# Twelve-layer decoder on one core: Hadamard layer's input levels as sums, cross attentions and latent layers in another order

## The reference, cut to what matters

```python
def _L0_xattn_ref(q, latent_kv, Wq, Wkv_expand, Wout):      # also layer 3
    qp = q @ Wq.T
    kv = latent_kv @ Wkv_expand.T
    k, v = jnp.split(kv, 2, axis=-1)
    # 16 heads of 32, causal softmax
    ...
    return out @ Wout.T

def _L0_ffn_ref(input, SU_ug, SU_dp, Wscale_ug, Wscale_dp, W_up, W_gate, W_down):
    x = fwht(x * SU_ug) / SCALE                             # Walsh-Hadamard transform over 512
    x_up = x @ W_up.T * (Wscale_ug[:INTER] * SCALE)
    x_gate = x @ W_gate.T * (Wscale_ug[INTER:] * SCALE)
    x = jax.nn.silu(x_gate) * x_up
    x = fwht(x * SU_dp) / SCALE                             # and over 2048
    x = x @ W_down.T * (Wscale_dp * SCALE)

def _L2_xattn_ref(hidden_q, kv_c, Wq, w_kc_q, w_kc_kv, W_qr, W_kr, Wo):   # layer 1 has no rope on q_big
    q_hk = (hidden_q @ Wq.T).reshape(Bv, Sv, H, K)          # 16 heads of 128
    q_big = jnp.einsum('bshk,hkq->bshq', q_hk, w_kc_q)      # 384 wide
    q_big = _apply_rope(q_big, ...)
    q_r = jnp.einsum('bshq,hqr->bhsr', q_big, W_qr)         # 64 wide
    k_r = jnp.einsum('bld,hdr->bhlr', kv_r, W_kr)
    attn = jax.nn.softmax(jnp.einsum('bhsr,bhlr->bhsl', q_r, k_r), axis=-1)
    ctx_c = jnp.einsum('bhsl,bld->bhsd', attn, kv_r)
    ctx_lat = jnp.einsum('bhsd,hkd->bhsk', ctx_c, w_kc_kv)
    return ctx_lat.transpose(0, 2, 1, 3).reshape(Bv, Sv, H * K) @ Wo.T
```

## Time and profile before

| | us |
|---|---|
| median of 3 runs (lowest to highest) | 3270.27 (3262.78 to 3283.12) |
| the profiled execution | 3272.31 |
| its span in the trace | 3270.4 |
| TensorE busy | 2955.3 |
| VectorE busy | 1426.4 |
| ScalarE busy | 1000.5 |
| GpSimd busy | 552.1 |
| mean granted clock of TensorE | 0.945 |

### The profile page before, as it was taken

How to read it: one execution, slowest core, us unless ns; L and a number is a source line. 1 busy time by engine, 2 the same in 40 slices (tenths; PEclk the granted TensorE clock), 3 DMA queues, 4 the chain that set the end, 5 groups by cost and what they waited for, 6 DMA issues and landing times.

```text
span 3270.4 us, 37436 instructions
## 1 busy us (share of the span) xinstructions
PE 2955.3 (90%) x14612; PEld 1853.2 (57%) x14612; DVE 1426.4 (44%) x2772; ACT 1000.5 (31%) x2925; POOL 552.1 (17%) x509
## 2 busy tenths in 40 slices
PE   8899989999999999998997898989999878888888
PEld 4455555555666656676553454545445646666666
DVE  5620276103655566202466655655465671111104
ACT  2210162101633343221442222222144613333331
POOL 0000020000200000241122211200000205655540
PEclk9899989999899999999998998999899879999998
DMA  4011101100011101584000001011001016754456
GB/s 161 15 50 45 65 27 66 46 29 0 22 38 45 45 36 49 204 298 140 17 22 24 21 25 33 17 39 39 19 27 59 11 57 225 254 195 150 131 149 149
DMA packets 65716, 249.11 MB, mean 76 GB/s; under 512 B 26394, under 2 KB 28442, under 8 KB 53604
## 3 DMA queue, kind: packets, MB, share of 16 engines
q1 hardware_dynamic: 30816, 177.88, 16.5%
q0 software_dynamic: 31344, 65.30, 6.0%
q10 hardware_dynamic: 3380, 3.53, 0.4%
HBM read 274.53 MB, written 42.13 MB: 97 GB/s over the span
## 4 chain that ended last, share of the span: by engine, by line
PE 71%; DVE 13%; ACT 7%; DMA 3%; another core or an unknown queue 3%; issue 1%; POOL 1%; SPq 0%; POOLq 0%; ACTq 0%; DVEq 0%
PE P L986 29%; PE P L990 12%; PE P L1357 9%; ACT A L1493 4%; PE P L1234 4%; PE P L996 4%; PE P L1252 3%; PE P L1225 2%; PE P L998 1%; DVE A L1957 1%; DVE A L1956 1%; DVE A L1955 1%; DMA A<-outputs 1%; PE P L1215 1%
## 5 line engine op out<-in xcount | busy, mean ns | idle before, releaser
L986 PE MATMUL P<-A,W 128*128 128x400 f32 x1680 | 611.5, 503 | 4.7 <-DVE A L1734 4.1
L1418 ACT ACTIVATE A<-P 128x400 f32<-128x400 f32 (+6 forms) x541 | 284.0, 537 | 688.8 <-PE P L998 204.6
L986 PEld LDWEIGHTS P<-A,W 128*128 128x128 f32 x1680 | 318.8, 192 | 243.0 <-issue 7.4
L986 PE MATMUL P<-X,W 128*128 128x400 f32 x816 | 311.3, 519 | 9.2 <-DMA W<-weights 8.5
L2212 DVE TENSOR_TENSOR A<-P,A 128x128 f32<-128x128 f32 (+1 forms) x141 | 44.9, 318 | 558.8 <-ACT A L1627 498.3
L2272 POOL TENSOR_TENSOR A<-A,small 100x1600 f32<-100x1600 f32 x32 | 91.6, 2862 | 1127.9 <-DVE small L1823 1127.9
L996 PE MATMUL P<-C,A 128*128 128x128 f32 (+5 forms) x1505 | 220.3, 270 | 41.5 <-POOL A L2272 18.0
L1493 ACT ACTIVATE A<-A,small 100x100 f32<-100x100 f32 (+1 forms) x640 | 229.2, 373 | 31.7 <-DVE small L1818 31.7
L986 PEld LDWEIGHTS P<-X,W 128*128 128x128 f32 x816 | 158.6, 197 | 130.3 <-issue 22.6
L996 PEld LDWEIGHTS P<-C,A 128*128 128x128 f32 (+5 forms) x1505 | 175.6, 147 | 92.4 <-issue 48.0
L990 PE MATMUL P<-A,W 128*128 128x400 f32 x496 | 207.0, 499 | 0.0
(11 more groups left out here) (278 smaller groups left out, 4390.9 us busy)
## 6 DMA issues: line engine op xcount, KB each, us to landing
W<-weights SPq DMA_DIRECT2D x60, 1024.0 KB, 4.8
A<-experts SPq DMA_DIRECT2D x16, 1536.0 KB
W<-experts SPq DMA_DIRECT2D x28, 768.0 KB
KT<-experts SPq DMA_DIRECT2D x15, 768.0 KB
...
```

Source lines behind the costliest of these rows:

```text
L986: self.e.matmul(out, a, b, start=i == 0, stop=False)
L1418: self.e.activation(out, in_, ACT.Copy).then_inc(*self.of(*item))
```

## The change

Sublayers 1 and 10: keys and queries of half 0 stand first, beside the previous sublayer's tail; keys and queries of half 1 and the value projections are filling in the pipeline. Some copies go to VectorE. The tail of sublayers 0 and 9 gets another order, and their filler matmuls at `norm_scale` of half 0 are left out. Sublayer 1's squares get a place of their own in memory.

Sublayer 2: the input's transform across the four blocks is made by eight VectorE sums and differences (`crossed`), which leaves one matmul for each block and half (`spread`). The signs go to ScalarE. Half 0 is made before half 1 is centred. `butterfly` becomes 16 steps of two instructions, by quarters of the columns, between the `fglu` steps.

Sublayers 4 and 7: steps of a turn stand half ahead of `mturn` and half behind `mscores`, and in 7 a table says which stand in which turn, so that a group's last preparations lie in the next group's first turns. `mfold`'s copy goes from VectorE to ScalarE.

```diff
         c = self.attention_sub(n, pre)
+        if n == 1:
+            self.norm_of(c, c.Z, self.ar(14592, 4, T))
...
-                    lambda m, h: c.K[:, m, hs(h)], lambda m, h: "act", piece=(pre, "kv"), clear=lambda h: c.before)
-        c.before = [("o", n - 1, 3, 0)]
+                    lambda m, h: c.K[:, m, hs(h)], lambda m, h: "act" if h == 0 or m % 2 else "dve", piece=(pre, "kv"))
...
+    def by_vector(self, c, b):
+
+        return c.n in (1, 10) and b % 2 == 1
...
-        c.B1, c.B2, c.H = self.ar(0, 16, 512), self.ar(8192, 16, 512), self.ar(8192, 16, T)
-        c.XS, c.XH = self.ar(16384, 4, T), self.ar(20992, 4, T)
+        c.B1, c.B2, c.H = self.ar(0, 16, 512), self.ar(24192, 16, 128), self.ar(8192, 16, T)
+        c.XS, c.X2, c.XH = self.ar(8192, 4, T), self.ar(11392, 4, T), self.ar(20992, 4, T)
...
-        return ([("norm_add", c, 0), ("norm_centre", c, 0), None, ("norm_add", c, 1), ("norm_scale", c, 0), ("norm_centre", c, 1)],
-                [None, None, ("norm_scale", c, 1)])
+
+        first = [("norm_add", c, 0), ("norm_centre", c, 0), None, ("norm_add", c, 1), ("norm_scale", c, 0)]
+        if c.n == 1:
+            return first, [("norm_centre", c, 1), ("norm_scale", c, 1)]
+        if c.n in (0, 9):
+            return first, [None, ("norm_centre", c, 1), None, None, None, ("norm_scale", c, 1)]
+        return first + [("norm_centre", c, 1)], [None, None, ("norm_scale", c, 1)]
...
-        yield from self.projection(c.kp, (tail, []))
-        values = self.values_steps(c)
-        yield from values
-        yield from self.projection(c.qp, halves=(0,))
-        return (yield from self.attention(c, self.turns_of([("proj", c.qp, m, 1) for m in range(4)], [])))
+        keys, queries = ([[("proj", p, m, h) for m in range(4)] for h in range(2)] for p in (c.kp, c.qp))
+        yield from beside(keys[0] + queries[0], tail)
+        return (yield from self.attention(c, self.turns_of(keys[1] + queries[1], self.values_steps(c))))
...
+        def plain_turns(g, left):
+            rest = (back(g - 1, 1) if g else left) + (plain(g + 1) if g < 3 else [])
+            share = -(-len(rest) // 5)
+            now = back(g, 0)
+            turns = {t: rest[share * (t - 1):share * t] for t in range(1, 6)}
+            return turns, {4: [("ofold", c, g)], **{t: [now[t - 5]] for t in range(5, 9)}}
...
+        def rotated_turns(g):
+
+            late = lambda h: [h[2][3], h[3][3]]
...
+                    more = {1: q[:2], 2: [b[0], q[2]], 3: [b[1], q[3]], 4: [f[0], b[2], k[0], q[4]], 5: [b[3], q[5]],
...
+            now = back(g, 0)
+            return turns, {7: [("ofold", c, g)], 8: now[:2], 9: now[2:]}
...
-            rest = behind + (group(g + 1) if g < 3 else [])
-            share = -(-len(rest) // (NB if c.roped else 5))
-            now, behind = back(g, 0), back(g, 1)
+            within, behind = rotated_turns(g) if c.roped else plain_turns(g, left)
             for t in range(NB + 2):
-                for i, name in ((2, "mvalues"), (1, "mturn"), (0, "mscores")):
-                    if 0 <= t - i < NB:
-                        if i == 1:
-                            yield from rest[:share]
-                            rest = rest[share:]
-                        yield name, c, g, t - i
-                if t == (7 if c.roped else 4):
-                    yield "ofold", c, g
-                for _ in range(2 if c.roped else 1):
-                    if t >= (8 if c.roped else 5) and now:
-                        yield now.pop(0)
-            yield from rest
-            yield from now
-        yield from beside(behind, first[:3] + [None] + first[3:])
+                if t >= 2:
+                    yield "mvalues", c, g, t - 2
+                steps = within.get(t, [])
+                n = (len(steps) + 1) // 2
+                yield from steps[:n]
+                if 0 <= t - 1 < NB:
+                    yield "mturn", c, g, t - 1
+                if t < NB:
+                    yield "mscores", c, g, t
+                yield from steps[n:]
+                yield from behind.get(t, [])
...
     def l0_ffn(self, c, tail):
-        tail = list(tail)
-        for g in (2, 3, 0, 1):
-            if g == 0:
-                yield from (s for s in tail if s)
-                tail = []
-            for k in range(4):
-                yield "wd_had", c, g, k
-                if k % 2 and tail:
-                    s = tail.pop(0)
-                    if s:
-                        yield s
-        yield "signs", c
-        yield from self.projection(c.xh)
-        yield "butterfly", c
-        yield from (("fglu", c, f, h) for f in range(16) for h in range(2))
+        wd = lambda g: [("wd_had", c, g, k) for k in range(4)]
+        spread = lambda h: [("spread", c, m, h) for m in range(4)]
+        yield "signs", c, 0
+        yield "crossed", c, 0
+        yield tail[0]
+        yield from wd(2)
+        yield from wd(3)
+        yield from spread(0)
+        yield tail[1]
+        yield "scales", c
+        yield "signs", c, 1
+        yield "crossed", c, 1
+        yield from wd(0)
+        yield from wd(1)
+        yield "fglu", c, 0, 0
+        yield "fglu", c, 1, 0
+        yield from spread(1)
+        levels = [("butterfly", c, q, lev) for q in range(4) for lev in range(4)]
+        rest = [("fglu", c, 0, 1), ("fglu", c, 1, 1)] + [("fglu", c, f, h) for f in range(2, 16) for h in range(2)]
+        yield from beside(rest, [None, None] + levels)
...
-        elif h == 0 and c.n < 11:
+        elif h == 0 and c.n not in (0, 9, 11):
...
+    def spread(self, c, m, h):
+
+        P = self.take(("proj", ("xh", 2), m, h), ("ev", ("xh", 2), m, h))
+        self.wait_ge(self.at("crossed", h))
+        self.e.matmul(P[:, 0:H2], self.c["had"], c.XS[:, m, hs(h)], start=True, stop=True).then_inc(*self.of("proj", ("xh", 2), m, h))
...
+    def signs(self, c, h):
+        for i in range(4):
+            self.wait_ge(self.at("x", 1, h, i) or self.at("x", 1, h))
+            self.e.activation(c.XS[:, i, hs(h)], self.k.x[:, i, hs(h)], ACT.Copy,
+                              scale=self.c["su"][:, i:i + 1]).then_inc(*self.of("xs", h, i))
...
+    def mfold(self, c, p):
+        self.wait_ge(self.at("fold", "m", c.n, p))
+        if p >= 2:
+            self.wait_ge(self.at("fold", "e", c.n, p - 2))
+        self.copy(c.MH[:, p % 2, :], self.ps("fold", "m", c.n, p)[:, 0:128], "mh", c.n, p)
...
-    def signs(self, c):
-        for i in range(4):
-            for h in range(2):
-                self.wait_ge(self.at("x", 1, h))
-                ins = self.e.tensor_scalar(c.XS[:, i, hs(h)], self.k.x[:, i, hs(h)], self.c["su"][:, i:i + 1], None, ALU.mult)
-                if i == 3:
-                    ins.then_inc(*self.of("xs", h))
-
-    def butterfly(self, c):
-        src, dst = c.B1, c.B2
-        self.wait_ge(self.at("wd", 1, 3))
-        self.wait_ge(self.at("wd", 1, 2))
-        for lev in range(4):
-            s = 1 << lev
-            for base in range(0, 16, 2 * s):
-                a, b = src[:, base:base + s, :], src[:, base + s:base + 2 * s, :]
-                self.e.tensor_tensor(dst[:, base:base + s, :], a, b, ALU.add)
-                i = self.e.tensor_tensor(dst[:, base + s:base + 2 * s, :], a, b, ALU.subtract)
-            last = ("turned",) if lev == 3 else ("level", lev)
-            i.then_inc(*self.of(*last))
-            self.wait_ge(self.at(*last))
-            src, dst = dst, src
+    def crossed(self, c, h):
+
+        XS, X2 = c.XS[:, :, hs(h)], c.X2[:, :, hs(h)]
+        self.wait_ge(self.at("ev", ("o", 1), 3, 1))
+        self.wait_ge(self.at("xs", h, 3))
+        self.e.tensor_tensor(X2[:, 0::2], XS[:, 0::2], XS[:, 1::2], ALU.add)
+        self.e.tensor_tensor(X2[:, 1::2], XS[:, 0::2], XS[:, 1::2], ALU.subtract).then_inc(*self.of("crossing", h))
+        self.wait_ge(self.at("crossing", h))
+        self.e.tensor_tensor(XS[:, 0:2], X2[:, 0:2], X2[:, 2:4], ALU.add)
+        self.e.tensor_tensor(XS[:, 2:4], X2[:, 0:2], X2[:, 2:4], ALU.subtract).then_inc(*self.of("crossed", h))
...
+    def butterfly(self, c, q, lev):
+
+        s, cols = 1 << lev, slice(128 * q, 128 * q + 128)
+        pairs = lambda a: a.rearrange("p (n two s) c -> p n two s c", two=2, s=s)
+        full, part = c.B1[:, :, cols], c.B2[:, :, :]
+        src, dst = (pairs(full), pairs(part)) if lev % 2 == 0 else (pairs(part), pairs(full))
+        if lev:
+            self.wait_ge(self.at("level", q, lev - 1))
+        else:
+            self.wait_ge(self.at("wd", 1, 3))
+            self.wait_ge(self.at("wd", 1, 2))
+            if q:
+                self.wait_ge(self.at("level", q - 1, 3))
+        a, b = src[:, :, 0], src[:, :, 1]
+        self.e.tensor_tensor(dst[:, :, 0], a, b, ALU.add)
+        i = self.e.tensor_tensor(dst[:, :, 1], a, b, ALU.subtract)
+        i.then_inc(*self.of("level", q, lev))
```

More of the change, by code:

```diff
@@ L777, in mla @@
         first, last = self.norms(c)
         tail = list(tail)
-        ahead = group(0)
```

(9 more changed lines are left out.)

66 lines of the change are left out of this document (38 added, 28 removed).

## The result

The changed kernel takes **3167.5 us** (median of 4 runs, 3163.4 to 3176.9); the kernel before took 3266.5 in the same comparison. The ratio is 0.969, with a 95% interval of 0.965 to 0.973. The prediction was 3173, within 3142 to 3212.

The account below looks back on a forecast made before the run. TensorE, busy 90% of the span, was taken as the bound, with VectorE counting only where TensorE waits for it. Savings of 63 + 10 + 11 + 11 + 2 = 97 us gave a median of 3173 us, range 3142 to 3212.

Parts of the forecast that it names:

- Sublayer 7, 63 less: Sublayer 7: 518 us instead of 582, as fold mostly stops waiting for GpSimd; 35 to 79 less at the ends.
- The walk through group 0: Sublayer 7, group 0: fold by fold idle times, plus 5 us for transposes and values; about 15 us.
- the floor of matmuls at full clock: Sublayer 7: 510.2 us busy at clock 0.95 leaves 485 us of matmuls at full clock.
- Groups 1 and 2: Sublayer 7: 2 us of waits each by the bank ring; they would take 121 to 122 us.
- half of the 25 us of waits with a full clock: Sublayer 7's best end: clock never lower and half the waits, given as 79 us less.
- Sublayer 2, 10 less: Sublayer 2: 16.1 us of matmuls removed, less new waits at its head and 2 for clock; 4 to 14 less.
- The waits by hand: Sublayer 2's head: wd_had waits 1.5 us, spread 3.0, the first fglu 2.9; 7.4 in all.
- Sublayers 1 and 10, 11 less in each: Cross attentions: head 16.9 us shorter, partly given back in the pipeline; 2 to 14 less in each.
- Sublayer 4, 2 less: Sublayer 4: ScalarE is free 1.6 us sooner for mfold's copy, which efold awaits; 6 less to 3 more.
- The second: Rival: VectorE's turn becomes the bound of sublayer 7, 35 us less there; 69 less in all, 3201 us; chance 0.15.
- The fourth: Rival: the bank ring locks TensorE and VectorE in sublayer 7's groups 0 to 2; 27 us more, 3299 to 3300; chance 0.02.
- The sixth: Rival: without filler ahead, each cross attention's pipeline stays at the lower clock, some 35 us more each; 3243 us; chance 0.02.

Follow-up runs that it names:

- e1: Kernel before with only the new order of sublayer 7: 3206.4 us for 3264.2, ratio 0.982.
- e4: Kernel before with only the new Hadamard layer (sublayer 2): 3247.2 us, ratio 0.996.
- e9: The changed kernel again, unaltered, as the measure for later runs: 3163.0 us for 3258.7, ratio 0.970.
- e8: Changed kernel with filler ahead of sublayers 1 and 10 back, sublayer 2's signs and mfold's copy on VectorE again: 3081.6 us, ratio to before 0.972.
- e7: Changed kernel with two extra pairs of VectorE copies in each batch of sublayer 7: sublayer 7 takes 553.0 us, ratio to before 0.980.
- e6: Changed kernel with one extra pair of VectorE copies in each batch of sublayer 7: sublayer 7 takes 533.5 us, ratio to before 0.972.

## Why the prediction was right

The sum was 97 less; the medians give 99. The windows of the five sublayers give 93, and the interval of the ratio is 14 us to either side, so the nearness to 2 us is partly luck; that each term is within 4 us of its window is not. Term by term:

- **Sublayer 7, 63 less:** 59 (58 in e1 from 581.0). The walk through group 0 gave fold waits of 0.4, 2.1, 5.2, 0.0 and 2.9; they are 0.2, 2.1, 5.1, 0.0 and 3.3. Its other waits are 6.9, for 5 and the 1.4 of `keyed`. Total idle time is 29.0 for 25, and behind stalls slow clock costs 5 (493.2 busy at 0.99) for 8; the floor of matmuls at full clock was then 488, not 485 (510.2 x 0.95, with a clock rounded to 0.01, is only good to 3). Groups 1 and 2 wait 3.1 each, for 2; that they would take 120 to 124 us held for group 2 (124.2), not for group 1 (128.9), which has 14 matmul records more: I had scaled the mean of both to full clock. Two slips don't touch the forecast: 582 less 518 is 64 and not 63 (the length between the writes of x is 581.0), and half of the 25 us of waits with a full clock would have been 84 less, not 79.
- **Sublayer 2, 10 less:** 8 in the first profile, 9 to 10 on one chip in e1 to e4. The waits by hand were 1.5, 3.0 and 2.9; they are 1.34, 2.68 and 2.92. Slow clock cost some 4 us in the first profile (285.5 busy, for 298.0 - 16.1 = 281.9) and 2 in e9, for 2. Butterfly stayed hidden.
- **Sublayers 1 and 10, 11 less in each:** 12 (12.2 and 11.6; 11 to 14 over the runs). The head was 16.0 by hand and is 16.2. The pipeline was mis-sized in its shape: two of its turns are 10.5 and 9.7 us long (from 393.80 to 404.26 to 413.92), where I had 7 to 8, and the later ones hold ScalarE's 6.6 to 7.1. In sum it gives back 4.6 for 5.9.
- **Sublayer 4, 2 less:** 2.4, all by the place of `mfold`'s copy (e8).
- **Rivals.** The second, VectorE as the bound of every turn, had 0.15 and deserved less: e7 shows groups 1 and 2 with room for more than twice the slack that I counted. Where VectorE is felt is group 0 (e6, e7). The fourth would be slower from (424 + 34)/24 - 13 = 6.1 us of waits a turn, not 5.8. The sixth, a pipeline that stays at the lower clock without filler, falls: its clock rose from 0.90 to 0.96. What lifted it isn't shown by a run. The 3.9 us wait and 17 us of thin head are gone, but the head was at 0.95 and is at 1.00, so most of the gain lies in the pipeline itself, which got 9.7 us of keys and values. The Trainium skill ("TensorE: Matmul & The Clock Gate", "What's actually happening") says that activity releases the throttle; the trace agrees in that 0.90 became 0.96 with these matmuls in it.
